# Two-layer vision tower on one core: half of the linear attention's scores masked through ScalarE and GpSimd, an earlier load of the fourth unit's pixels, positions issued by ScalarE, and new order tables

## What is computed

```python
h = patchify(x) @ W_proj.T + b_proj + pos_emb             # (32, 36, 256)

n = layernorm(h)                                          # layer 0, linear attention, 16 heads of 16
q, k, v = elu(n @ Wq.T) + 1, elu(n @ Wk.T) + 1, n @ Wv.T
num = einsum('bhtd,bhtde->bhte', q, cumsum(einsum('bhtd,bhte->bhtde', k, v), axis=2))
den = einsum('bhtd,bhtd->bht', q, cumsum(k, axis=2))
h = h + (num / maximum(den, 1e-6)) @ Wo.T

n = layernorm(h)                                          # layer 0, feed-forward with LoRA
gate = softmax(n @ router_w.T)                            # 8 experts of rank 8
h = h + n @ base_w.T + 2 * einsum('bsr,erd,bse->bsd', n @ lora_A, lora_B, gate)

n = layernorm(h)                                          # layer 1, softmax attention
h = h + softmax(causal((n @ Qw) @ (n @ Kw).T / 16)) @ (n @ Vw)

n = layernorm(h); p = shift_by_one_token(n)               # layer 1, mixing
h = h + sigmoid(mix(mu_r, n, p) @ W_r.T) * (relu(mix(mu_k, n, p) @ W_k.T) ** 2 @ W_v.T)
```

## Time and profile before

| | before |
|---|---|
| median of 3 runs | 192.59 us |
| the three runs | 193.06, 190.46, 192.59 us |
| the profiled execution | 191.7 us |
| its span on the core | 189.7 us |
| mean granted TensorE clock | 0.988 |

### The profile page before, as it was taken

How to read it: one execution, slowest core, us unless ns; L and a number is a source line. 1 busy time by engine, 2 the same in 40 slices (tenths; PEclk the granted TensorE clock), 3 DMA queues, 4 the chain that set the end, 5 groups by cost and what they waited for, 6 DMA issues and landing times.

```text
span 189.7 us, 4662 instructions
## 1 busy us (share of the span) xinstructions
PE 176.2 (93%) x1640; PEld 149.5 (79%) x1640; DVE 137.0 (72%) x430; ACT 89.4 (47%) x246; POOL 81.5 (43%) x147
## 2 busy tenths in 40 slices
PE   6986899999999999999999999999999989986992
...
DVE  6577059777787997796897786989794786637731
...
PEclk9999789999999999999999999999999999999998
...
DMA packets 20004, 11.70 MB, mean 62 GB/s; under 512 B 12318, under 2 KB 19982, under 8 KB 19982
## 3 DMA queue, kind: packets, MB, share of 16 engines
...
## 4 chain that ended last, share of the span: by engine, by line
PE 71%; DVE 8%; SPq 6%; DMA 5%; issue 3%; POOL 3%; ACT 2%; POOLq 0%; DVEq 0%; ACTq 0%
PE single L577 10%; PE quad L577 9%; PE single L702 8%; PE quad L679 5%; PE single L693 5%; PE single L787 4%; PE single L792 4%; PE single L608 4%; PE single L749 4%; PE single L720 4%; PE single L752 4%; DMA xT<-in_x_dram 3%; DMA hB<-hT 2%; PE single L776 2%; PE single L761 2%
## 5 line engine op out<-in xcount | busy, mean ns | idle before, releaser
L473 POOL TENSOR_TENSOR ln_rs<-ln_ve,mhalf 108x1 f32<-108x1 f32 (+2 forms) x40 | 22.4, 564 | 46.4 <-DVE ln_ve L1033 46.2
L1127 DVE TENSOR_TENSOR S<-quad,mask 108x864 f32<-108x864 f32 (+1 forms) x22 | 21.8, 1022 | 2.0 <-PE quad L679 1.7
L577 PE MATMUL single<-wp_hi,x_hi 128*108 128x256 f32 (+1 forms) x66 | 19.9, 302 | 1.2 <-DVE x_lo L987 1.0
L577 PE MATMUL single<-wp_hi,x_lo 128*108 128x256 f32 (+1 forms) x66 | 19.2, 291 | 0.0
L577 PE MATMUL single<-wp_lo,x_hi 128*108 128x256 f32 (+1 forms) x66 | 19.1, 289 | 0.0
L608 PE MATMUL single<-ident,ln_xn 108*128 108x108 f32 (+2 forms) x80 | 15.2, 272 | 4.1 <-ACT ln_xn L852 2.1
L608 PEld LDWEIGHTS single<-ident,ln_xn 108*128 108x128 f32 (+2 forms) x80 | 9.8, 143 | 8.5 <-issue 4.3
L528 POOL TENSOR_TENSOR v<-v,hB 108x256 f32<-108x256 f32 (+1 forms) x11 | 8.8, 800 | 16.3 <-DVE v L1230 16.3
L486 POOL TENSOR_TENSOR x_lo<-xT,x_hi 128x648 fp32r<-128x648 f32 (+1 forms) x8 | 12.1, 1514 | 4.3 <-ACT x_hi L815 4.3
L577 PEld LDWEIGHTS single<-wp_hi,x_hi 128*108 128x108 f32 (+1 forms) x66 | 11.8, 178 | 2.5 <-issue 2.5
L749 PEld LDWEIGHTS single<-F,G 128*128 128x128 f32 x88 | 11.1, 191 | 1.5 <-DVE hT L1189 0.8
...
## 6 DMA issues: line engine op xcount, KB each, us to landing
xT<-in_x_dram SPq DMA_DIRECT2D x7, 324.0 KB, 5.9
...
xT<-in_x_dram ACTq DMA_DIRECT2D x1, 324.0 KB, 6.2
...
```

Of the source, the lines that this page charges most:

```text
L473: nc.gpsimd.tensor_tensor(L.rs[0:t, j:j + 1], L.ve[0:t, j:j + 1], mhalf[0:t, :], ALU.pow).then_inc(L.rstd_done, 1)
L577: ins = nc.tensor.matmul(out_ap, lhs, rhs, start=(start and n == 0), stop=(stop and n == len(terms) - 1))
L1127: nc.vector.tensor_tensor(S[0:t, j, 2 * h:2 * h + 2, 0:4 * t].rearrange("p r (e t) -> p r e t", e=4), quad[0:t, 2 * h:2 * h + 2, 0:4 * t]. ...
```

## The change

1. **Scores.** VectorE masks only banks 0 and 1 (`e.u`, one instruction a unit). ScalarE copies banks 2 and 3 unmasked from `quad` to `S` (`ea.u`, `f_raw`), and GpSimd multiplies that half by the mask in place (`em.u`, `f_mask`). The next user of `quad` waits for `e.u` and `ea.u`; `av.u` waits for `e.u` and `em.u`.
2. **Start.** SP issues the pixels of unit 3 ahead of Wk, Wv, Wq and those of unit 4 right behind them, and `XS` becomes 6. The bias and the positions are issued by ScalarE, behind a small copy that follows the load of its function table.
3. **Layernorm 1** joins `VLN`: `ap1` moves from ScalarE to VectorE, and GpSimd's bias step for it goes.
4. **Buffers.** `z`, `zT` and `at` shrink from four slots to two, with the waits that this needs.
5. **Tables.** All order tables and the banks are new.

```diff
-VLN = (2, 3)
+VLN = (1, 2, 3)
...
-    idle.20 tok.0 tok.1 tok.2 idle.3 tr0.0 idle.3 tok.3 tr0.1 tok.4 tr0.2 k.0 k.1 q.0 q.1 tr0.3 fold.0 tok.5
+    idle.20 tok.0 tok.1 tok.2 tok.3 idle.4 tok.4 tr0.0 tr0.1 idle.1 tok.5 tr0.2 k.0 k.1 q.0 q.1 tok.6 v.0 v.1
...
-        XS, XN, UN, QS, FN, VS = 5, 3, 4, 2, 5, 5
+        XS, XN, UN, QS, FN, VS = 6, 3, 4, 2, 5, 5
...
-        at = sb("at", [P, UN, KT, TMAX])
+        at = sb("at", [P, BN, KT, TMAX])
...
             load_x(sp, 2)
-            for k in range(3):
-                sp.dma_start(pos[k * NTOK:(k + 1) * NTOK, :], a["L0_tok_pos_emb"]).then_inc(s["pos_loaded"], 16)
-            row(sp, bproj, "L0_tok_b_proj", "bproj_loaded")
+            load_x(sp, 3)
             for n in SPLIT:
                 load_w(n, w_raw[n], w_loaded[n])
+            load_x(sp, 4)
...
-            for u in range(3, XS):
+            for u in range(5, XS):
                 load_x(sp, u)
...
+            def f_mask(u):
+                t, j = T[u], u % 2
+                pool.wait_ge(s["s_raw"], u + 1)
+                v = S[0:t, j, 2:4, 0:4 * t].rearrange("p r (e t) -> p r e t", e=4)
+                nc.gpsimd.tensor_tensor(
+                    v, v, mask01[0:t, 0:t].rearrange("p (o n t) -> p o n t", o=1, n=1).to_broadcast([t, 2, 4, t]),
+                    ALU.mult).then_inc(s["s_masked_pool"], 1)
...
                 if held4[0]:
                     pe.wait_ge(*held4[0])
+                    if held4[0][0] is s["s_raw"]:
+                        pe.wait_ge(s["s_masked"], held4[0][1])
...
-                pe.wait_ge(s["s_masked"], 2 * u + 2)
+                pe.wait_ge(s["s_masked"], u + 1)
+                pe.wait_ge(s["s_masked_pool"], u + 1)
...
             load_wp(act, 1)
             load_x(act, 1)
+
+            act.wait_ge(s["zeros_ready"], 1)
+            copy(rdc[:, 0:1], restart[:, 1:2])
+            row(act, bproj, "L0_tok_b_proj", "bproj_loaded")
+            for k in range(3):
+                act.dma_start(pos[k * NTOK:(k + 1) * NTOK, :], a["L0_tok_pos_emb"]).then_inc(s["pos_loaded"], 16)
...
+            def f_raw(u):
+                t, j = T[u], u % 2
+                if u >= 2:
+                    act.wait_ge(s["av_mm"], u - 1)
+                if u == 0:
+                    act.wait_ge(s["w_lo_ready"], len(SPLIT))
+                act.wait_ge(s["s_mm"], u + 1)
+                copy(S[0:t, j, 2:4, 0:4 * t], quad[0:t, 2:4, 0:4 * t]).then_inc(s["s_raw"], 1)
```

More of the change, by code:

```diff
@@ L49 @@
 XLV = 3
-VLN = (2, 3)
+VLN = (1, 2, 3)
 BANKS = {
-    "fold": "1",
-    "tok": "01202201113",
-    "tr0": "31303202201",
-    "dc": "1313",
-    "av": "33312010213",
-    "atv": "12321021212",
-    "sc": "00103321131",
-    "pt": "21230120130",
-    "pv": "02311322313",
-    "tr3": "12300330212",
-    "rk": "21303132003",
-    "ou": "12223233121",
-    "wo": "010300210",
-    "tr1": "023303310",
-    "ffn": "231303210",
-    "zt": "103312230",
-    "lo": "022011110",
-    "tr2": "232120320",
+    "fold": "3",
+    "tok": "01230313022",
+    "tr0": "12021200132",
+    "dc": "0301",
+    "av": "12333130210",
+    "atv": "12202232102",
+    "sc": "03212131231",
+    "pt": "10011221230",
+    "pv": "00122003113",
+    "tr3": "22230000212",
+    "rk": "31203202003",
+    "ou": "02213303121",
+    "wo": "321201010",
+    "tr1": "121333120",
+    "ffn": "030033301",
+    "zt": "111103311",
+    "lo": "222320233",
+    "tr2": "010321221",
@@ L86 @@
-    pt.9 pt.10 pv.9 pv.10 rk.7 rk.8 tr3.9 ou.7 tr3.10 ou.8 rk.9 rk.10 ou.9 ou.10
+    idle.20 tok.0 tok.1 tok.2 tok.3 idle.4 tok.4 tr0.0 tr0.1 idle.1 tok.5 tr0.2 k.0 k.1 q.0 q.1 tok.6 v.0 v.1
+    tr0.3 dc.0 s.0 fold.0 s.1 tr0.4 tr0.5 tr0.6 tok.7 av.0 av.1 db.0 tok.8 wo.0 k.2 k.3 q.2 q.3 tr1.0 tok.9
+    ffn.0 v.2 v.3 dc.1 zt.0 v.4 lo.0 tr0.7 tr0.8 s.2 tr0.9 tok.10 tr2.0 db.1 atv.0 av.2 s.3 wo.1 sc.0 k.4 k.5
+    pt.0 q.4 av.3 tr1.1 pv.0 q.5 wo.2 ffn.1 tr0.10 v.5 v.6 dc.2 v.7 tr1.2 tr3.0 ffn.2 zt.1 s.4 lo.1 rk.0 zt.2
@@ L87 @@
+    atv.8 rk.5 rk.6 ou.5 pt.7 sc.8 ou.6 tr2.8 pv.7 pt.8 atv.9 pv.8 atv.10 sc.9 tr3.7 sc.10 tr3.8 pt.9 pt.10
+    pv.9 pv.10 rk.7 rk.8 tr3.9 ou.7 tr3.10 ou.8 rk.9 rk.10 ou.9 ou.10
 """
 ACT_ORDER = """
[L89 to L91 removed]
```

129 lines of the change are left out of this document (65 added, 64 removed).

## The result

The changed kernel takes 199.21 us (median of 4 runs, 198.55 to 202.03) and the kernel before, beside it, 191.53 us (190.31 to 193.06). The ratio is 1.039, with a 95% interval of 1.026 to 1.051: slower, where 189.0 us was forecast and 193.0 was the top of the range. The profiled execution of after is its slowest (202.03 us, a span of 200.3, mean granted clock 0.98); its runs at a clock of 1.00 have spans of 196.8 and 196.9.

The account below looks back on a forecast made before the run. TensorE was taken to bound the kernel, with a hole at the start. From 191.7 us: -3.1 (start), +0.9 (first scores), +0.6 (VectorE held), -1.3 (late order) = 188.8, stated as 189.0; range 185.5 to 193.0.

Parts of the forecast that it names:

- What bounds the kernel: Whole run: TensorE bounds it, busy 97.15 of 98 us in the middle, with a hole at the start from 18 us.
- Unit 3's pixels early: Start: unit 3's pixels land at 12.4 us, so tok.3 is ready at 14.7, 1.9 us before TensorE wants it.
- Positions issued by ScalarE: Start: the copy and four issues end at 5.3 us, ahead of `wp_hi` at 5.58; costed at nothing, cover 0.3 us.
- Up to k.0: Start: k.0 at 26.3 us with six toks done instead of five; 3.1 us gained, bounds 0.9 and 4.6.
- First scores: After the start: s.1 waits 0.9 us for unit 8's late pixels and the copy `ea.0`, bounds 0 and 3.
- Masks: Middle: moving half the masks off VectorE to ScalarE copies and GpSimd products costs zero, bounds -1 to +3 us.
- VectorE held by GpSimd: Middle: masks hold VectorE's instructions 7 us, as much as its relief; 0.6 us added for waits, bounds 0 and 5.
- Layernorm 1: `ap1`: VectorE takes 4.4 us and ScalarE sheds 5.4, off the path; zero.
- The late order: Late program, before tr3.6: unit 4's rk and ou fill TensorE's holes, 1.3 us gained, bounds 0 and 2.6.
- the slower rival: Middle: GpSimd's masks hold VectorE's instructions so long that its load stalls TensorE; 195.9 us, chance 0.12.
- The new gates take it back: Rival, start: ap0.2 behind unit 7, unit 8 two us late, clock down again; 192.1 us, no change, chance 0.18.

Follow-up runs that it names:

- the positions on SyncE: Kernel before with unit 3's pixels ahead of the weights and tok.3 right behind tok.2, positions and bias still issued by SyncE: 190.0 us, ratio 0.997.
- the short mask in after: Kernel after with GpSimd's mask cut to 8 columns, the rest of that half left unmasked: 193.55 us, ratio 1.014.
- the masks aside in after: Kernel after with GpSimd's masks writing a spare tile, value products waiting only for the ScalarE copy, half the scores unmasked: 196.54 us, ratio 1.032.
- The experiments with SyncE's positions: Kernel before with unit 3's pixels first and positions on SyncE; then 28 fillers; then also gates moved: 190.0, 191.79 and 191.93 us.
- the short mask there: Kernel before with the mask change alone, in the old order, and GpSimd's mask cut to 8 columns: 189.75 us, ratio 0.996.

## Why the prediction was wrong, point by point

*What bounds the kernel* was right: the middle is TensorE's, and a middle with more than 3 us of waits was named as a sign that the prediction is wrong. It has 9.7 us of idle time.

*Unit 3's pixels early.* The hole at 18 us went, as said. But tok.3's copy ran at 15.17 and not at 12.4: it waits for tok.0 to free its slot, and tok.0 was late and at half clock. The landing itself was sized well: with the positions on SyncE the copy ran at 12.72.

*Positions issued by ScalarE* is a step that failed. ScalarE's issues were hidden (`wp_hi` starts at 5.29), but I priced only the engine that issues and not the transfers: on a second queue they run beside unit 0's pixels, which were copied at 9.51 instead of 8.46. (Unit 3's own transfer, 324 KB, starts earlier there too, in the place of the positions; its share in the delay was not separated.) The idle time before tok.0 is 3.46 us in place of 0.97, and the clock halves: tok.0 alone takes 3.88 us on the chain of waits.

*Up to k.0.* Predicted 26.3 with six toks, measured 29.08: 27.01 - 29.08 + 2.19 = 0.1 us gained, where 3.1 was in the sum. The fall of the clock behind the late tok.0 makes 1.5 us of this: in three kernels with the same start (all masks on VectorE, the short mask in after, the masks aside in after) the wait ahead of tok.0 was 2.12 to 2.75 us, the clock stayed at 1.00, and k.0 ran at 27.5 to 27.7. The next gate was not unit 5's pixels either, whose copy ran at 19.40 where 21.2 was predicted, but the first layer norms. `pos` stood behind `xl.3` on GpSimd, so hF.0 ran at 18.86 and not at 15.5, VectorE's low half of Wv took 1.41 us beside `x_lo` on GpSimd (0.66 before), and ap0.0 ran at 23.64. The experiments with SyncE's positions show that even without the late tok.0 the gates behind, ap0.1 and then unit 4's pixels, leave 0.1 to 1.8 us, and hardly any of it is in the ratios. The mechanism of the hole was right, its size in the sum was not.

*First scores.* s.1 waits 0.75 us (0.9 predicted): right.

*Masks*, priced at zero. The lengths were right (2.045 us on GpSimd against 2.03, 0.887 on ScalarE against 0.9), and so was the statement that VectorE's masks lie off the path, for the old order: the short mask there shows it (0.996). In the new order it was wrong, by 4.4 us. The price of zero for 2 us on GpSimd was wrong too: with the masks alone they cost 4.3 us of TensorE's middle, above the bound of 3. I looked only at the cover between s.u and av.u. I didn't price what queues behind the mask on GpSimd, the roots of three layer norms and `xd`, each on the way to a product of TensorE. In the kernel after itself this queue did not bite: VectorE waits for the roots and `xd` no longer than with the short mask.

*VectorE held by GpSimd* is where the 4.0 us of the masks' length in after stand, and the step that failed is "I add 0.6 us for waits that surface, bounds 0 and 5". I set 7 us of holding against 7 us of relief in VectorE's load and took them to cancel. But VectorE's load fell (74.14 us for 80.75), and the cost came all the same, because the held instructions are on the way from each layer norm and from each gate to TensorE: `ln_xn` and `gate` last 6.8 us longer than with the short mask, and TensorE waits 2.0 us more for `ln_xn` and 1.3 more for `z`. That 6.8 is close to my 7 was luck. Of "some 30 such instructions" I counted those with two SBUF inputs, and the holding in after falls on `ln_xn` and `gate`, with one SBUF input each, for a whole mask (2.02 and 2.24 us). The Trainium skill (SBUF — State Buffer, "Who interferes with whom") does name them: `tensor_scalar` can enter the two-port modes when its operands meet their conditions, and an instruction in such a mode contends with GpSimd for the whole instruction. The two rows agree with it. I used only the sentence on two inputs. With the masks alone in the old order nothing is held, and they cost 4.3 us all the same, through the queue and TensorE's own wait for the mask.

*Layernorm 1* at zero was right (0.999 with ap1 moved alone).

*The late order* filled its holes but gained less than the 1.3 us in the sum: of waits like those of 0.56 and 0.24 us of the earlier trace rows one of 0.17 is left from 150 to 175 us, but others opened (1.39 us at 136.61, 0.98 at 181.24), and from 134 us on TensorE waits 3.4 us in after and 4.1 in before. The same tables also re-ordered the middle, and the sum had no term for that. This is the step that failed with the largest price: it costs 4.3 to 4.8 us, half of the loss. In the short-mask kernel those stalls are TensorE's waits for `ln_xn`, `F`, `qT` and `z`: the new order asks for them sooner than VectorE has them.

*The rivals.* The time came nearest to the slower rival (195.9, given 0.12), for a mechanism that is part of the truth. It put the loss down to VectorE's load, which in fact fell to 74 us of 98; the loss is latency. That the kernel with all masks on VectorE in the new order is as slow (200.4) shows that the rival alone is not the cause. "The new gates take it back" did happen at the start, with 0.1 us left.

*Open.* Which of the moved steps of the new order cost the 4.3 to 4.8 us was not taken apart. That the masks' length acts by holding in the new order rests on the waits of two traces; no run of the new order has masks of 2 us that hold nothing.
